# A 363-product edit to a chain of eight attention and feed-forward stages on one core: zero bf16 products in TensorE's queue at the changes of stage

## What is computed

```python
x = x + L0_xattn(layernorm(x), ctx, ctx, mask)    # a0: 16 heads
x = x + L0_ffn(layernorm(x))                      # m0: 64 experts, top 8, hidden 192, plus a shared one
x = x + L1_xattn(layernorm(x), ctx, mask)         # a1: one head
x = x + L1_ffn(layernorm(x))                      # local: 2 layers of windowed attention (8 heads) and GEGLU
x = x + L2_xattn(layernorm(x), ctx, ctx)          # a2: 16 heads
x = x + L2_ffn(layernorm(x))                      # m2: 8 experts, top 2, hidden 1024, capacity 538
x = x + L3_xattn(layernorm(x), ctx)               # a3: 16 heads of 64
x = x + L3_ffn(layernorm(x))                      # m3: 8 experts, top 2, hidden 1024
```

## Time and profile before

| | |
|---|---|
| median of 3 runs | 2209.79 us (2208.41 to 2211.33) |
| profiled execution, its own time | 2211.68 us |
| its span | 2209.9 us |
| PE busy (x 12891 instructions) | 2042.1 us, 92% |
| weight loads of PE | 1526.9 us, 69% |
| DVE, ACT, POOL busy | 1098.7, 937.1, 613.7 us |
| mean granted TensorE clock | 0.955 |

### The profile page before, as it was taken

One profiled execution on the slowest core, in us unless ns is written; L12 is line 12 of the kernel. 1 busy time (PEld: TensorE's weight loads), 2 busy tenths in 40 slices (PEclk: granted clock), 3 DMA queues, 4 the chain that ended last, 5 costly groups with the idle time before them and its releaser, 6 DMA issues. The chain is left out here.

```text
span 2209.9 us, 39358 instructions
## 1 busy us (share of the span) xinstructions
PE 2042.1 (92%) x12891; PEld 1526.9 (69%) x12891; DVE 1098.7 (50%) x4126; ACT 937.1 (42%) x2965; POOL 613.7 (28%) x553
## 2 busy tenths in 40 slices
PE   7999999788999898899989799799997999599999
PEld 4776688555666555566645478578885677599998
DVE  5785344567777432777743368612222566322121
ACT  4564133255777420677742044322221666232332
POOL 0677466322222100222200002312223122221222
PEclk9999899789999999999999889899998999799999
DMA  8702799776700200000000181111122701466662
GB/s 287 296 20 64 235 338 333 207 234 214 299 12 11 68 1 27 18 10 11 11 8 1 62 286 43 43 35 32 32 59 54 249 35 40 166 184 184 175 184 56
DMA packets 162510, 255.35 MB, mean 116 GB/s; under 512 B 37484, under 2 KB 125967, under 8 KB 161270
## 3 DMA queue, kind: packets, MB, share of 16 engines
q1 hardware_dynamic: 132886, 224.62, 29.3%
q0 software_dynamic: 29424, 28.21, 7.2%
HBM read 165.95 MB, written 101.04 MB: 121 GB/s over the span
## 5 line engine op out<-in xcount | busy, mean ns | idle before, releaser
L2819 ACT ACTIVATE m3e_ht<-m3e_h_bank,m3w_b 128x128 f32<-128x128 f32 x312 | 89.2, 368 | 192.4 <-PE m3e_h_bank L2791 192.4
L3438 ACT ACTIVATE la_probs<-la_probs,la_nb,la_invnorm 128x256 f32<-128x256 f32 x256 | 150.2, 594 | 0.2
L2802 PE MATMUL m3e_y_bank<-m3w_w,m3e_ht 128*128 x624 | 141.0, 379 | 0.0
L2980 ACT ACTIVATE m2e_ht<-m2e_h_bank,m2w_b 128x270 f32<-128x270 f32 x128 | 62.3, 487 | 179.3 <-PE m2e_h_bank L2942 179.3
L981 POOL DMA_INDIRECT m_xbuf<-m0w_rows,m0w_slots x128 | 125.7, 982 | 39.7 <-issue 36.9
L2766 POOL DMA_INDIRECT out<-m3e_y,m3e_dest x39 | 60.4, 1548 | 239.0 <-DVE m3e_y L2854 225.1
L2802 PEld LDWEIGHTS m3e_y_bank<-m3w_w,m3e_ht 128*128 128x128 f32 x624 | 115.7, 190 | 14.1
L2917 POOL DMA_INDIRECT m_sum<-m2e_y,m2e_dest x48 | 70.2, 1462 | 197.2 <-DVE m2e_y L3028 186.2
L2831 DVE COPY m3e_xt<-m3e_turned_bank 128x256 f32<-128x256 f32 x39 | 16.6, 425 | 218.0 <-PE m3e_turned_bank L2779 218.0
L2942 PE MATMUL m2e_h_bank<-m2e_xt,m2w_w 128*128 128x270 f32 x512 | 121.9, 396 | 0.0
L2954 PE MATMUL m2e_y_bank<-m2e_ht,m2w_w 128*128 128x270 f32 x512 | 119.4, 391 | 0.0
(11 more groups left out here) (522 smaller groups left out, 4850.6 us busy)
## 6 DMA issues: line engine op xcount, KB each, us to landing
m3w_w<-in_m_w SPq DMA_DIRECT2D x32, 1024.0 KB, 6.5
m_xbuf<-all_zeros SPq DMA_DIRECT2D x38, 528.0 KB, 6.0
m2w_w<-in_m_w SPq DMA_DIRECT2D x16, 1024.0 KB, 12.7
m3e_w<-in_m_w SPq DMA_DIRECT2D x15, 1024.0 KB, 6.2
m0w_wgu<-in_m_gu SPq DMA_DIRECT2D x16, 768.0 KB, 14.3
m_xbuf<-all_zeros SPq DMA_DIRECT2D x16, 576.0 KB, 13.6
m0w_down<-in_m_down SPq DMA_DIRECT2D x23, 384.0 KB, 14.9
m_sum<-all_zeros SPq DMA_DIRECT2D x16, 512.0 KB
```

The lines of the kernel that those rows point to most:

```text
L2802: last = nc.tensor.matmul(y_ps[t % 2][0:R, 0:D], h_t[t % 2][:, c, :], ahead.w2[:, bass.ts(e, 1), c, :].rearrange("p o f -> p (o f)"), star ...
L2819: last = nc.scalar.activation(h_t[t % 2][:, 4 * half + i, :], h_ps[t % 2][half][:, i * R:(i + 1) * R], m.act, bias=ahead.b1[:, bass.ds(e * ...
L3438: last = nc.scalar.activation(probs[u][:, hh, :], probs[u][:, hh, :], ACT.Exp, bias=nb[u][:, hh:hh + 1], scale=inv_norm[u][:, hh:hh + 1], ...
```

## The change

A block `k.filler` of 128 x 128 bf16 zeros is set once at the start. `fill(k, bank, n)` puts n products of it with itself, broadcast to 512 columns, into TensorE's queue; their results go to a bank that nobody reads before it is written anew. They wait for nothing of their own. Calls stand at the end and at the start of stages, in the first steps of a2 and a3, in the last three steps of a2, in the second step of a1, and before the last four tiles of the two local feed-forwards. In m0 a wait for the last `y_copied` stands in front of them. Nothing is removed or moved.

```diff
@@ -89,6 +89,12 @@
 
 class Shared:
     pass
+
+
+def fill(k, bank, n):
+
+    for _ in range(n):
+        k.nc.tensor.matmul(bank[:, 0:4 * P], k.filler[:, :], k.filler[:, :].unsqueeze(1).broadcast_to([P, 4, P]), start=True, stop=True)
 
 
 class Scope:
@@ -762,11 +768,18 @@
                     nc.tensor.matmul(pos_ps, before16[:, :], chosen[t % 2][:, :], start=True, stop=False, skip_group_check=True)
                     nc.tensor.matmul(pos_ps, k.ones[:, :], sofar[t % 3][:, :], start=False, stop=True, skip_group_check=True).then_inc(counted, 1)
 
-                every_step(T, (0, turn), (3, turn_p), (3, mix), (4, return_x), (1, lambda t: score(t, 0)), (1, lambda t: score(t, 1)),
+                fill(k, out_ps, 16)
+
+                def fill_first(t):
+                    if t == 0:
+                        fill(k, out_ps, 4)
+
+                every_step(T, (0, turn), (0, fill_first), (3, turn_p), (3, mix), (4, return_x), (1, lambda t: score(t, 0)), (1, lambda t: score(t, 1)),
                            (4, route_x), (5, count), (1, lambda t: score(t, 2)))
                 pe.wait_ge(summed, T)
                 pe.wait_ge(picking, 3 * (T - 1) + 1)
                 nc.tensor.matmul(pos_ps, k.ones[:, :], sofar[T % 3][:, :], start=True, stop=True, skip_group_check=True).then_inc(totalled, 1)
+                fill(k, turned_ps, 52)
         old.close()
     k.fold_ahead.ctx.close()
 
@@ -1916,6 +1929,7 @@
 
             @block.tensor
             def _(pe):
+                fill(k, out_ps, 36)
                 pe.wait_ge(h.loaded, 64)
                 pe.wait_ge(ahead.router_in, 16 * ahead.router_n)
                 pe.wait_ge(started, 1)
@@ -2037,9 +2051,18 @@
                     nc.tensor.matmul(pos_ps, before16[:, :], chosen[t % 2][:, :], start=True, stop=False, skip_group_check=True)
                     nc.tensor.matmul(pos_ps, k.ones[:, :], sofar[t % 3][:, :], start=False, stop=True, skip_group_check=True).then_inc(counted, 1)
 
-                every_step(T, (0, turn), (2, lambda t: turn_p(t, 0)), (3, turn_o), (2, lambda t: turn_p(t, 1)), (4, return_x),
-                           (2, lambda t: value(t, 0)), (3, project), (0, query), (2, lambda t: turn_p(t, 2)), (2, lambda t: value(t, 1)),
-                           (5, count), (4, route_x), (0, score), (2, lambda t: value(t, 2)))
+                def fill_first(t):
+                    if t < 2:
+                        fill(k, out_ps, 3)
+
+                def fill_last(t):
+                    if t >= T - 3:
+                        fill(k, out_ps, 3)
+
+                every_step(T, (0, turn), (0, fill_first), (2, lambda t: turn_p(t, 0)), (3, turn_o), (2, lambda t: turn_p(t, 1)), (4, return_x),
+                           (2, lambda t: value(t, 0)), (3, project), (0, query), (0, fill_first), (2, lambda t: turn_p(t, 2)), (2, lambda t: value(t, 1)),
+                           (5, count), (4, route_x), (5, fill_last), (0, score), (2, lambda t: value(t, 2)))
+                fill(k, out_ps, 26)
         old.close()
 
 
@@ -2396,6 +2419,7 @@
                     nc.tensor.matmul(bank[:, 0:4 * P], none[:, :], none[:, :].unsqueeze(1).broadcast_to([P, 4, P]), start=True, stop=True)
 
                 pe.wait_ge(warm, 1)
+                fill(k, fa_ps[1], 36)
                 for step in range(T + 3):
                     if 0 <= step - 1 < T:
                         score(step - 1)
@@ -2404,6 +2428,8 @@
                     if step in projects:
                         keys_values3(projects[step])
                         keep_warm(fa_ps[1])
+                    if step == 1:
+                        fill(k, fa_ps[1], 10)
                     if step < T:
                         turn(step)
                     if step < 5:
@@ -2415,6 +2441,7 @@
                         fold_values3(folds[step])
                 pe.wait_ge(fold3_copied, A3_PAIRS)
                 pe.wait_ge(vw3_copied, A3_PAIRS)
+                fill(k, fa_ps[1], 24)
         old.close()
 
 
@@ -2600,6 +2627,8 @@
                 fold_queries()
                 fold_values()
                 project_heads()
+                pe.wait_ge(y_copied, npair)
+                fill(k, y_ps[0], 5)
 
             @block.scalar
             def _(act):
@@ -2769,6 +2798,7 @@
 
             @block.tensor
             def _(pe):
+                fill(k, y_ps[0], 17)
                 pe.wait_ge(ahead.weights_in, 16 * ahead.weights_n)
 
                 def turn(t):
@@ -2921,6 +2951,7 @@
 
             @block.tensor
             def _(pe):
+                fill(k, turned_ps[0], 16)
                 pe.wait_ge(ahead.weights_in, 16 * ahead.weights_n)
 
                 def turn(h):
@@ -2967,6 +2998,7 @@
 
                 every_step(NH, (0, turn), (1, up), (2, lambda h: back(h, 0)), (1, down),
                            (2, lambda h: None if h == NH - 2 else back(h, 1)))
+                fill(k, turned_ps[0], 26)
 
             @block.scalar
             def _(act):
@@ -3475,6 +3507,7 @@
                 for st in (turned, projected, qk_turned, scored, p_turned, mixed, inv_turned, made, forward.turned):
                     pe.sem_inc(st.sem, 2 * st.n)
                 pe.wait_ge(ready, 2)
+                fill(k, score_ps[0], 4)
 
                 def turn(t):
                     if l == 0:
@@ -3494,6 +3527,7 @@
 
                 def project_q(t):
                     if t == 0:
+                        fill(k, score_ps[0], 3)
                         pe.wait_ge(lo.attention_in[l], 32)
                     pe.wait_ge(copied.sem, copied.at(t, "copied"))
                     pe.wait_ge(qk_copied.sem, qk_copied.at(t - 1, "q"))
@@ -3606,6 +3640,7 @@
                 forward.turn(pe, 3, k_ps)
                 turn_inv(LAST)
                 output(LAST)
+                fill(k, c_ps, 14)
 
 
 def local_feed_forward(nc, k, d, l, lo, forward):
@@ -3761,8 +3796,10 @@
                                 forward.turn(pe, t, t_ps[t % 2])
                             if g >= 1 and c % 2 == 0:
                                 down(4 * (g - 1) + c - 2)
+                fill(k, t_ps[0], 8)
                 for t in range(T - 4, T, 2):
                     down(t)
+                fill(k, t_ps[0], 6 if l == 0 else 10)
 
 
 def local_layers(nc, k, d):
@@ -3824,6 +3861,7 @@
         k.folded = {}
         k.iota, k.before, k.ones = s.sb("iota", [P, 64]), s.sb("before", [P, P]), s.sb("ones", [P, P])
         k.minus_half = s.sb("minushalf", [P, 16])
+        k.filler = s.sb("filler", [P, P], BF16)
         k.zeros = s.sb("zeros", [P, 4 * PAYLOAD])
         k.token, k.spare = s.sb("token", [P, T]), s.sb("spare", [P, 2])
         k.constants_in, = s.lasting_sems("constantsin", 1)
@@ -3850,6 +3888,7 @@
                 nc.vector.memset(k.ones3[:, :], 1.0)
                 nc.vector.memset(k.ones[:, :], 1.0)
                 nc.vector.memset(k.minus_half[:, :], -0.5)
+                nc.vector.memset(k.filler[:, :], 0.0)
 
         k.heads = Heads(k, d["a2"])
         k.second_inputs, k.third_inputs = d["a1"], d["a3"]
```

## The result

| | before | changed | ratio, 95% interval |
|---|---|---|---|
| median of the runs beside each other | 2210.0 us (2208.4 to 2212.4) | 2193.2 us (2190.4 to 2197.8) | 0.9924 [0.9907, 0.9941] |
| profiled execution, own time / span | 2211.68 / 2209.9 us | 2193.20 / 2191.4 us | |
| mean granted clock, profiled run | 0.955 | 0.985 | |

The change saves 16.8 us by the medians (2210.0 - 2193.2) and 18.5 us by the two profiled executions. The forecast was 2188 in a range of 2178 to 2202.

What follows compares the result with a forecast made beforehand. The prediction took dense TensorE work at half clock behind waits between stages as the bound (199 us at 1.2 GHz). Nine seam terms summed to 22.6 us, giving 2187.2 by the median; it predicted 2188, range 2178 to 2202.

Steps and rivals of the forecast that it cites:

- 3: Local attention to feed-forward in layer 0: fillers fit the gap, dense half-rate work returns half its time; net 3.1 us.
- 5: Attention 1 to feed-forward 1: dense work at full clock behind a filled gap, shorter window; net 1.6 us.
- Seam 4: Feed-forward 0 to attention 1: gains in the feed-forward's last tiles and attention's projections, less late ends and starts; net 3.0 us.
- a2's start (6): Feed-forward 1 to a2: the largest term, 7.6 us from full clock, reduced for filler cost and waits to 6.3 us.
- 7: a2 to m2: 3.1 us from full clock, less a late block end taken as 2.2; net 0.9 us.
- 9: a3 to m3: 1.7 us from full clock, less 1.3 for late ends; net 0.4 us.
- a3's start (8): m2 to a3: fillers fit the gap, the first tile's dense scores run at full clock; net 3.0 us.
- a1's start (1): m0 to a1: 3.0 us from full clock, less 0.5 for five fillers before the block's end; net 2.5 us.
- a1 to the first local attention (2): a1's end to the first local attention: full clock on its half-rate work, limited by DVE's table scaling; net 1.8 us.
- A: Stage starts are paced by DMA, DVE and ACT, so earlier TensorE only waits longer: 2199 us; chance 0.15.
- B: Fillers cost more than 0.21 us each: about 2226 us at 0.38, 2271 at 0.43; chance 0.09.
- C: Nothing moves: gains at dense seams and late block ends cancel, 2205 to 2214 us; chance 0.06.

Runs made afterwards that it cites:

- e9: e5 with the remaining short waits also filled in a1's second and third tiles and the last steps of a2 and a3: 2185.1 us, ratio 0.9890.
- e6: The kernel before with only the fillers of a2's start (10 at feed-forward 1's end, 36, 12 in the first two steps): 2204.5 us, ratio 0.9980.
- e7: The changed kernel without the fillers at a1's end, in the local attentions and feed-forwards, except the ten at feed-forward 1's end: 2202.3 us, ratio 0.9955.
- e2: The changed kernel without the fillers of a2's start (10 at feed-forward 1's end, 36, 12 in the first two steps): 2200.8 us, ratio 0.9958.
- e3: The changed kernel without the 9 + 26 fillers at a2's end and the 16 at m2's start: 2195.6 us, ratio 0.9939.
- e8: The changed kernel without the 52 fillers at a3's end and the 17 at m3's start: 2192.7 us, ratio 0.9921.
- e4: The changed kernel, fillers cut at m0's, a2's, a3's and feed-forward 0's ends, raised at a1's end and m2's start, four moved before `ready`: 2190.5 us.
- e10: The changed kernel itself measured and profiled again, nothing altered: 2192.8 us, ratio 0.9929.
- e1: The changed kernel with all 363 fillers kept, each using 3 of the 128 rows: 2263.9 us, ratio 1.0249.
- e11: The same kernel as e4, measured and profiled again beside the changed kernel: 2191.5 us, ratio 0.9918.
- e5: e4 with nine fillers before and five behind the last product group of the shared expert in a0: 2189.7 us, ratio 0.9909.

## Why the prediction was right, and where it was off

**The bound and the price.** Right: fillers cost 0.216 us, the half-rate stretches behind the large waits are gone but for the first local attention's, and the clock came to 0.985 where 0.98 was expected. The change returned 0.76% [0.59%, 0.93%] of the time and e9 1.10% [0.92%, 1.29%], with half-rate stretches still left in it. The Trainium skill, "TensorE: Matmul & The Clock Gate" (Part 1, "What's actually happening"), puts the ramp penalty at under 1% of a typical kernel's span, from which the prediction had estimated 2199 beside its sum. What e9 got back lies at that figure, its interval begins below it, and it is not the whole of the penalty, so here the figure is met or passed.

**The dense seams (3, 5, half of 4).** Feed-forward 0 is 4.1 us shorter, with 3.1 + 1.75 - 0.5 = 4.35 foreseen; its block ends 0.6 us behind Vector, taken as 0.5. This one repeats in every profile. Feed-forward 1 is 1.6 us shorter, as foreseen, but e6 has the same 126.0 us without fillers there, and e7 lost 3.5: the agreement to a tenth is luck. Seam 4's second half, 1.65, agrees with attention 1's 1.8 us in number, but e6 and e7 have 251.0 us without its fillers, so it is not shown.

**a2's start (6).** Right: from the block's start to Vector's last work 171.75 us became 165.43, 6.3 less. Inside the stage the fifth tile is 6.1 us earlier than before, and e2 and e6 measured 7.6 and 5.7 by the medians.

**The seams with late ends (7, 9).** The 29 fillers took 8.32 us, inside 7.9 to 9.6, and the block ended 6.4 us behind Vector. SP's first load for m2 followed it, not the scatters, as foreseen. From Vector's last work in a2 to m2's first transposes are 1426.80 - 1416.17 = 10.6 us against 1439.32 - 1430.61 = 8.7: 1.9 late, 2.2 taken. Net 1.1 or 3.4 by e3 and the two profiles of the changed kernel (0.9 foreseen), and at a3 to m3 nothing that shows by e8 (0.4).

**a3's start (8).** Right. The first twelve score products of a3 take 4.35 us where they took 6.94; this is their row before:

```profile
1710.18 6.94 PE L704 MATMUL a_score_bank<-a3w_fold,a_xnt 128*128 128x462 f32 x12
```

Up to Vector's last work a3 lost 3.1 us, 3.0 taken. The end of the ninth tile's copy into `a_xnt`, from a3's start, is 76.1 us before and 75.9 in e6, and 73.3 to 73.4 us in all ten profiles with the fillers: 2.5 to 2.9 us, every time.

**a1's start (1).** Not shown, though the number agrees. a1 lost 2.9 us between the two profiles, 3.0 taken. But with fillers at its start it is 82.6 to 85.5 us over ten profiles, and 85.5 again in e2; without them it is 85.5 us before and 81.7 in e6, the shortest of all, with 23.9 us at half clock from 413.3 us on. So what the fillers are worth here, and whether anything, stays open. m0 was 1.1 us longer and not 0.5. Tensor's end behind Scalar gives 0.5 of it, as taken (e4, without the five fillers, is 0.6 shorter); the rest is already there in Scalar's last work (167.6 us against 167.1), ahead of the fillers, and e3 has its 167.2 with all five.

**The term that was mis-sized: a1 to the first local attention (2).** Taken as 1.8, it was 0.7 us in one profile and 0.5 in the other. Three more profiles have the same code there (e2, e3, e8), with 250.4, 251.3 and 251.1 us, so the changed form lies between 249.9 and 251.3, and the form without fillers between 250.1 and 250.9 (before, e6, e7). What the runs show in place of 1.8 us is nothing that can be told from zero. The step that failed is "four more stand behind the wait for `ready`: 0 to 0.85 us late", together with the half of 5.49 us that was to come back. It counted on the clock holding through that wait. The 24 in front ended at 497.3 and left 3.42 us of waiting for Vector, in which the clock fell. A window of the changed kernel:

```profile
499.90:503.30 3.40, 2.63 (x8) 1.30 (x9) 3.29 (x9) 0.00 (x0) 1.65 (x3) 0.50 0.06 6
```

So four fillers took 1.87 us on the path, and the first transposes came at 502.33, against 500.80 in the earlier trace rows. In e10 the wait was 2.31 us and the four ran at full clock, but the clock fell behind them, on the projections that were to gain:

```profile
503.20:506.60 3.40, 3.40 (x7) 1.33 (x5) 2.54 (x6) 0.37 (x1) 0.00 (x0) 0.50 0.10 11
```

All five profiles of this form have a stretch at half clock that starts between 497.0 and 503.2 us. e4 shows the other side: with 31 in front and the four ahead of the wait there is none, and att0 is 249.2 us in both profiles, 0.9 to 1.7 us below the form without fillers.

**The rest of the difference.** The seams sum to 22.6, the profiles to 18.5. Of the 4.1 us, 1.1 are seam 2, 0.7 are m0 with a1, and 1.9 are a0, where the change puts nothing: 244.3 us against 242.4. Over the kernels whose a0 is the same code it is 241.7 to 242.4 us in five profiles (before, e1, e3, e6, e8) and 244.1 to 244.7 in six; the longer ones have two stretches at half clock in their first 33 us, the shorter ones one or none. By then the difference is there: a tenth of Vector's instructions in a0 are done 42.4 to 43.3 us after its start in the shorter ones and 44.8 to 45.4 us in the longer. Kernels with fillers are among both, so the longer value is not bound to the change; but both kernels that were profiled twice gave it twice. What picks it stays open.

**How much of this was luck.** The terms that repeat in every profile are feed-forward 0, a2's start and a3's start: 13.5 us of the two profiles' 18.5 (4.1, 6.3 and 3.1), where 4.35, 6.3 and 3.0 were foreseen. m3 adds about one more. Of the others, the first local attention's was wrong, and a1's, attention 1's and feed-forward 1's agree in sum with stages that vary by as much in programs with the same code.

**Rivals.** A would have shown 2199 and late starts; a2's and a3's starts, with a DMA share of 1.02 to 1.09, gave their gain in full. Its price has a slip: it took half of seam 6 as 2.5 us, where half of 6.3 is 3.2, so it should have said 2198. At a1 and at the first local attention nothing contradicts A. B's price of 0.43 us a filler is real (e1), but not for products over all rows at full clock. C asked for late ends at most seams: there are four, of 0.5 to 6.4 us. The medians put trimming them at 1.4 to 2.7 us, with ranges that overlap.

## What to carry to other kernels

Look for stretches in which TensorE is busy and its granted clock is 0.50. Price a filler at the clock that it will find, not at full clock: here it cost 0.216 us at full and 0.43 at half. In front of a wait it is free as long as the wait is longer; behind the wait it is on the path. Long waits between stages are the easy part. The waits of 1 to 2 us in front of dense products gave more per filler: e9 has 60 more than e11 and is 6.4 us faster, where the change's 363 gave 16.8. Fillers over 3 rows did not hold the clock and those over 128 did. A claim on one stage that is smaller than some 4 us needs more than one profile of the same kernel, or a place inside the stage that repeats.

## What the runs showed of the hardware

- Zero products over 128 rows held the clock at 1.00 (the windows above); the same number over 3 rows did not (0.53 with PE busy for 14.40 of 14.40 us, clock 0.949 over the run).
- Short waits are enough for a fall: the half-rate stretch of 13.7 us at a0's end follows a wait of 1.97 us, and in e5 one of 6.8 us at 1863.6 follows waits of 0.51, 0.70 and 1.28 us. Filling the wait of 1.97 us took the first stretch away (none there in e5, 3.4 us in e9). The Trainium skill, "TensorE: Matmul & The Clock Gate" ("A second HAM failure mode: psum-queue depth-cycling"), tells of a kernel whose frequent short idles between groups of products made the clock swing; the stretches behind these waits agree.
- The same wait does not always bring the same fall. A timeline row of attention 1 in the changed kernel, and the same one in e10, which is the same kernel:

```profile
1100.38 3.60 PE L3569 MATMUL la_score_bank<-la_kt,la_qt 64*128 64x128 f32 x32 [2.20 <-DVE la_mx L3381]
```

```profile
1101.06 2.06 PE L3569 MATMUL la_score_bank<-la_kt,la_qt 64*128 64x128 f32 x32 [2.20 <-DVE la_mx L3381]
```

  The same 32 products behind the same wait of 2.20 us take 3.60 and 2.06 us. The windows there, in the same order, show the clock at 0.50 and at 1.00:

```profile
1100.60:1104.00 3.40, 3.40 (x33) 3.18 (x31) 2.09 (x10) 3.01 (x12) 0.00 (x0) 0.50 0.00 0
```

```profile
1100.40:1104.00 3.60, 2.94 (x36) 2.76 (x37) 2.96 (x15) 3.60 (x13) 0.00 (x0) 1.00 0.00 0
```

  With stages of equal code 1.5 to 3.6 us apart in two profiles of one kernel, this is the uncertainty under which every small term above stands.
